# State-space scan of a decoder block: units of 1024 columns in place of 512, overwritten in place

## The reference

```
# 1. Mamba (I = 512 channels, N = 16 states)
hs, gate = split(x @ in_proj_w.T);  u = silu(conv4(hs) + conv_b)
dt, B, C = rmsnorm of the parts of u @ x_proj_w.T;  dt = softplus(dt @ dt_proj_w.T + dt_proj_b)
h[t] = exp(dt[t] * A) * h[t-1] + dt[t] * u[t] * B[t]      # per channel and state
y[t] = sum over states of h[t] * C[t];  y = (y + u * D) * silu(gate);  out = y @ out_proj_w.T
# 2. mLSTM over ctx_1024, 4 heads, gates from cumulative sums, norm over each head
# 3. feed-forward graph of 6 nodes, each with edge matrices q, k, v and attention of 8 heads
q, k, v = ew * (nodes @ We + be);  nodes[c] = act_w * (attention(q, k, v) @ Wo) + q
```

## Time and profile before

| | us |
|---|---|
| median of 3 runs | 1309.74 (1309.69 to 1315.06) |
| the profiled execution | 1308.01 |
| its span, first to last instruction | 1306.2 |
| TensorE busy | 1098.0 (84%) |
| VectorE busy | 1053.6 (81%) |
| ScalarE busy | 720.6 (55%) |
| mean granted TensorE clock | 0.939 of 2.4 GHz |

### The profile page before, as it was taken

How to read it: one execution, slowest core, us unless ns; L and a number is a source line. 1 busy time by engine, 2 the same in 40 slices (tenths; PEclk the granted TensorE clock), 3 DMA queues, 4 the chain that set the end, 5 groups by cost and what they waited for, 6 DMA issues and landing times. The chain is left out here.

```text
span 1306.2 us, 27811 instructions
## 1 busy us (share of the span) xinstructions
PE 1098.0 (84%) x11504; PEld 822.0 (63%) x11504; DVE 1053.6 (81%) x1683; ACT 720.6 (55%) x1692; POOL 2.9 (0%) x10
## 2 busy tenths in 40 slices
PE   3845668988999899989988998899888988897886
PEld 2723445766676667666666666666666666676665
DVE  2289887799999999999999999999999889725112
ACT  1434532576657665776567556755576646444332
POOL 0000000000000000000000000000000000000000
PEclk9767775999999999999999999999999989999998
DMA  6440343004100410030112211030104000000000
GB/s 190 122 178 32 107 153 113 33 3 130 41 26 33 132 42 25 34 105 28 50 49 62 71 50 49 16 117 33 58 3 130 33 25 34 2 1 10 2 1 9
DMA packets 53710, 76.14 MB, mean 58 GB/s; under 512 B 15376, under 2 KB 38672, under 8 KB 53456
## 3 DMA queue, kind: packets, MB, share of 16 engines
q1 hardware_dynamic: 53584, 74.37, 17.9%
HBM read 63.60 MB, written 10.75 MB: 57 GB/s over the span
## 5 line engine op out<-in xcount | busy, mean ns | idle before, releaser
L979 DVE TENSOR_TENSOR_SCAN unit_buf<-dec,unit_buf 128x512 f32<-128x512 f32 x256 | 311.9, 1218 | 11.7 <-ACT dec L753 11.0
L753 ACT ACTIVATE dec<-dts,a_neg 128x254 f32<-128x254 f32 x512 | 225.6, 499 | 42.5 <-DVE unit_buf L979 37.3
L972 DVE TENSOR_TENSOR unit_buf<-dtus,bs 128x512 f32<-128x512 f32 x256 | 175.0, 686 | 6.3 <-DMA dtus<-dt_rows 2.5
L990 DVE TENSOR_TENSOR unit_buf<-unit_buf,cs 128x512 f32<-128x512 f32 x256 | 175.3, 685 | 0.5
L1087 DVE TENSOR_REDUCE mx<-heads 128x16 f32<-128x2048 f32 x48 | 109.2, 2276 | 50.1 <-PE heads L602 50.0
L487 PE MATMUL ps<-unit_buf,fold 128*32 128x256 f32 x1024 | 89.0, 420 | 52.4 <-DVE unit_buf L990 52.3
L825 ACT ACTIVATE pr<-heads 128x512 f32<-128x512 f32 x192 | 99.1, 603 | 49.0 <-PE heads L617 49.0
L571 PE MATMUL ps<-node,wq_f 128*128 128x256 f32 x384 | 93.6, 387 | 7.8 <-ACT node L840 7.8
L640 PE MATMUL heads<-node,we_f 128*128 128x256 f32 x384 | 94.7, 389 | 0.0
L647 PE MATMUL heads<-aT,wo_f 128*128 128x256 f32 x384 | 93.7, 387 | 0.9 <-DVE aT L1096 0.9
L581 PE MATMUL heads<-wv_f,node 128*128 128x256 f32 x384 | 91.8, 382 | 0.0
(11 more groups left out here) (178 smaller groups left out, 1777.8 us busy)
## 6 DMA issues: line engine op xcount, KB each, us to landing
dts<-dt_rows SPq DMA_DIRECT2D x32, 512.0 KB, 3.8
dtus<-dt_rows SPq DMA_DIRECT2D x32, 512.0 KB, 5.2
node<-in_w_edgeT SPq DMA_DIRECT2D x18, 256.0 KB, 3.6
dt_rows<-dt SPq DMA_DIRECT2D x32, 128.0 KB, 2.4
dt_rows<-th SPq DMA_DIRECT2D x32, 128.0 KB, 2.5
bs<-bc_rows SPq DMA_DIRECT2D x32, 128.0 KB, 4.6
cs<-bc_rows SPq DMA_DIRECT2D x32, 128.0 KB, 4.3
xin<-in_x SPq DMA_DIRECT2D x8, 256.0 KB, 6.2
```

The source lines that it names most:

```text
L753: last = fn(dec[k % 2][:, a, :, 1:L], dts[c % 2][:, blk, :].rearrange("p (b t) -> p b t", b=GB)[:, :, 1:L], ACT.Exp, scale=a_neg[:, c, blk ...
L972: v.tensor_tensor(inf[k % 2][:], dtus[c % 2][:, 2 * pair:2 * pair + 2, :], bs[:, q:q + 1, :].broadcast_to([P, 2, T]), ALU.mult).then_inc(s ...
L979: v.tensor_tensor_scan(hst[k % 2][:].rearrange("p a b -> p (a b)"), dec[k % 2][:].rearrange("p a b t -> p (a b t)"), inf[k % 2][:].rearran ...
L990: v.tensor_tensor(prd[(i * UNITS + k) % PRDS][:], hst[k % 2][:], cs[:, q:q + 1, :].broadcast_to([P, 2, T]), ALU.mult).then_inc(sig["outflo ...
```

## The change

A unit becomes all four blocks of one set: 4x256 = 1024 columns. There are 4 units a chunk and 16 a group. Input, states and product share one tile: feed writes `ring[k % 3]`, scan overwrites it with the states, weigh overwrites those with the product, and the fold reads it. So feed of unit k waits until the fold of unit k-3 is done, and the waits of scan and weigh for free buffers are gone. `unit` k on VectorE is now weigh k-1, feed k+1, scan k. ScalarE makes four instructions of decays for a unit; `dec` has two buffers of 1024 columns. The fold is one for each unit, with the same matmuls as one for two before. The four tables are new.

```diff
-CUNITS = NGRP * BLKS // 2
+CUNITS = NGRP
-PRDS = 5
+RING = 3
...
-    if _k >= 2 and _k % 2 == 0:
-        U_STEPS += [("u", "add", _k // 2 - 1)]
+    if _k >= 1:
+        U_STEPS += [("u", "add", _k - 1)]
...
-A_AT = [-90, -86, -76, -69, -62, -58, -57, -52, -44, -43, -42]
+A_AT = [-101, -88, -76, -75, -62, -58, -56, -52, -49, -43, -42]
...
-        dec = [sb(f"dec{j}", [P, 2, GB, L]) for j in range(2)]
-        unit_buf = sb("unit_buf", [P, 4 + PRDS, 2 * T])
-        inf, hst, prd = ([unit_buf[:, j].rearrange("p (a n) -> p a n", a=2) for j in slots]
-                         for slots in ((0, 1), (2, 3), range(4, 4 + PRDS)))
+        dec = [sb(f"dec{j}", [P, BLKS, GB, L]) for j in range(2)]
+        ring = [sb(f"ring{j}", [P, BLKS, T]) for j in range(RING)]
...
-                    after(sp, used, i - 1, UNITS - CUNITS + 2 * q + 2)
+                    after(sp, used, i - 1, UNITS - CUNITS + q + 1)
...
-            def add(i, j):
-                c, q = j // NGRP, j % NGRP
+            def add(i, k):
+                c, q = k // CUNITS, k % CUNITS
                 if q == 0:
                     after(pe, "y_read", i, c)
-                after(pe, "outflow", i, 2 * j + 2)
-                for k in (2 * j, 2 * j + 1):
-                    for a in range(2):
-                        r0 = SD * (k % 2 * 2 + a)
-                        last = mm(MY[r0:r0 + SD, 0:T], fold[:], prd[(i * UNITS + k) % PRDS][:, a, :],
-                                  start=(q == 0), stop=(q == NGRP - 1), tile_position=(0, r0))
+                after(pe, "outflow", i, k + 1)
+                for blk in range(BLKS):
+                    last = mm(MY[SD * blk:SD * (blk + 1), 0:T], fold[:], ring[(i * UNITS + k) % RING][:, blk, :],
+                              start=(q == 0), stop=(q == NGRP - 1), tile_position=(0, SD * blk))
...
                 after(act, "state", i, k - 1)
-                for a in range(2):
-                    blk = 2 * pair + a
-                    last = fn(dec[k % 2][:, a, :, 1:L],
+                for blk in range(BLKS):
+                    last = fn(dec[k % 2][:, blk, :, 1:L],
...
             def feed(i, k):
-                after(dve, "state", i, k - 1)
-                v.tensor_tensor(inf[k % 2][:], dtus[c % 2][:, 2 * pair:2 * pair + 2, :],
-                                bs[:, q:q + 1, :].broadcast_to([P, 2, T]), ALU.mult).then_inc(sig["inflow"], 1)
+                after(dve, "ysum", i, k - RING + 1)
+                v.tensor_tensor(ring[(i * UNITS + k) % RING][:], dtus[c % 2][:],
+                                bs[:, q:q + 1, :].broadcast_to([P, BLKS, T]), ALU.mult).then_inc(sig["inflow"], 1)
             def scan(i, k):
+                states = ring[(i * UNITS + k) % RING][:].rearrange("p k t -> p (k t)")
                 after(dve, "decay", i, k + 1)
                 after(dve, "inflow", i, k + 1)
-                after(dve, "outflow", i, k - 1)
-                v.tensor_tensor_scan(hst[k % 2][:].rearrange("p a b -> p (a b)"),
-                                     dec[k % 2][:].rearrange("p a b t -> p (a b t)"),
-                                     inf[k % 2][:].rearrange("p a b -> p (a b)"), 0.0, ALU.mult,
+                v.tensor_tensor_scan(states, dec[k % 2][:].rearrange("p k b t -> p (k b t)"), states, 0.0, ALU.mult,
                                      ALU.add).then_inc(sig["state"], 1)
             def weigh(i, k):
+                states = ring[(i * UNITS + k) % RING]
                 after(dve, "state", i, k + 1)
-                after(dve, "ysum", i, (k - PRDS) // 2 + 1)
...
+                v.tensor_tensor(states[:], states[:], cs[:, q:q + 1, :].broadcast_to([P, BLKS, T]),
+                                ALU.mult).then_inc(sig["outflow"], 1)
...
             def unit(i, k):
                 if k == 0:
                     feed(i, 0)
+                if k >= 1:
+                    weigh(i, k - 1)
                 if k + 1 < UNITS:
                     feed(i, k + 1)
-                if k >= 1:
-                    weigh(i, k - 1)
                 scan(i, k)
```

29 lines of the change are left out of this document (13 added, 16 removed).

## The result

The changed kernel takes 1314.53 us in the median of 20 runs (1312.73 to 1321.43), the kernel before 1309.77 in the same comparison: ratio 1.0038, interval 1.0028 to 1.0048. It is slower by 0.4%, within what the prediction called no change; forecast were 1286 us and a gain. The profiled execution took 1313.7 us.

What follows compares the result with a forecast made beforehand. VectorE, nearly full in six of eight periods, was taken as the bound. Savings of 17.4 us over six periods, 5.5 at the start and 1.0 in the last but one made 23.9 off 1308.0; median forecast 1286, range 1278 to 1294.

Steps and rivals of the forecast that it cites:

- The multiplies: On VectorE, merging two 512-column multiplications saves about 0.075 us by distance of starts; 32 merges a group, 2.4 us.
- the scan: On VectorE, a 1024-column scan takes 2310 ns; each merge saves 0.04 us, 0.7 us a group.
- the dependent start: VectorE instructions waiting for the scan just issued start 0.12 us later; fewer such places save 0.9 us a group.
- Rival B: VectorE's fixed instruction cost counts in full, 7.7 us a group, but TensorE's 133.0 us limit cuts: 1272 us; chance 0.12.
- In place at zero: VectorE scans overwriting their own tile cost nothing extra; bounds zero and 1.9 us a group, no gain expected.
- New waits, 1.1 us a group, at the ring: VectorE feeds wait for TensorE's folds to free one of three tiles, 1.0 us a group; wide units delaying TensorE, 0.1.
- Period 137.3-4.0+1.1 = 134.4: Steady period: VectorE's 4.0 us saving taken off in full, 1.1 us of new waits added; six periods give 17.4 us.
- TensorE's floor of 133.0: Steady period if VectorE never held TensorE up, with TensorE's own work and waits for ScalarE unchanged: 133.0 us.
- ScalarE at nothing: Four decay exponentials for one wide unit have the same cover from VectorE's work as before, so no cost.
- Start, -5.5: Before the first feed-forward: 6.0 us from wide units plus 2.5 from the norm, less 3 at weight preparations: 5.5 us less.
- C: Slower: the ring of three ties the engines together, 9.0 us of waits a group against 4.0 gained: 1334 us; chance 0.10.
- D: No change: new waits eat the gain in the periods, weight preparations eat the start's: 1308 us; chance 0.08.

Runs made afterwards that it cites:

- e15: Kernel before with input, states and product of each 512-column unit in one tile overwritten in place, nine tiles; order, tables, widths unchanged: 1306.3 us, ratio 0.9971 to before.
- e2: Changed kernel's wide units and ring of three, but at the slots of the four old tables: 1614.4 us, ratio 1.2328 to before.
- e1: Changed kernel, same order and tiles, with each of a unit's three VectorE instructions issued as two of 512 columns: 1329.7 us, ratio 1.0153 to before.
- e17: Kernel of e16 with each merged multiplication again as two of 512 columns, at the places the merge gave them: 1322.6 us, ratio 1.0085 to before.
- e3: Changed kernel with each scan over only the first 512 of its 1024 columns (work left out): 1295.4 us, ratio 0.9889 to before.
- e4: Kernel before with each scan over only the first 256 of its 512 columns (work left out): 1283.2 us, ratio 0.9791 to before.
- e9: Changed kernel with two dummy TensorE products ahead of each of two waits, the dt projection's second half and the last head's values: 1310.4 us, ratio 1.0030 to before.
- e11: Changed kernel with each of ScalarE's decays computed for only the first half of a sequence (work left out): 1310.1 us, ratio 1.0000 to before.
- e18: Kernel of e15 in a ring of four, with only the two weighings of a pair merged, at the second one's place: 1324.6 us, ratio 1.0103 to before.
- e6: Changed kernel with all four slot tables rewritten: feeds moved by 1 to 6 slots, two folds and the weight preparations later: 1328.7 us, ratio 1.0133 to before.
- e8: Changed kernel with one number of the mLSTM table changed, the last head's scores at slot 57 instead of 58: 1345.2 us, ratio 1.0270 to before.
- e10: Changed kernel with the weight preparations' slot table taken back to that of the kernel before: 1334.8 us, ratio 1.0184 to before.
- e16: Kernel of e15 in a ring of four, with the two multiplications of a pair of units merged to 1024 columns, scans narrow: 1315.4 us, ratio 1.0048 to before.

## Why the prediction was wrong

- *The multiplies, the scan, the dependent start:* right. Starts 1.13 apart; scan 2285 ns for 2310 forecast, the dependent product 2.32 us behind it (550.54 to 552.86). Behind a wide scan an instruction that doesn't wait starts after 2.20 us, for 2.22 forecast. VectorE's busy time fell 3.4 us a period, for a forecast of 4.0. Rival B, the fixed cost in full, falls with the starts. By the Trainium skill ("VectorE: DVE Perf Modes", section on the TRN2 errata) the fixed cost lies between instructions, and the starts would be 1.22 apart, an estimate from its figure; the trace has 1.13 and disagrees.
- *The page's busy sum, -54:* it fell 29.3. I took it for a sum of durations; where starts overlap ends it is not, it is their union. The three groups' own sums fell by 662.2-603.6 = 58.6 us.
- *In place at zero:* not slower, right; but e15 is 0.6 us a period faster (0.4 between periods without a fall of the clock), and the dependent start is the difference that its trace shows, even without wider units.
- *New waits, 1.1 us a group, at the ring:* wrong in kind. No feed waited for a fold, and in e2, which is 304 us slower, only one did, 2.1 us. What the ring and the pairs cost lay in the order, with the falls of the clock that it brings: 3.0 us a period in e1, 2.9 in e17 against e15.
- *Period 137.3-4.0+1.1 = 134.4:* **this step failed.** It took VectorE's saved time off the period in full because VectorE was nearly full. e3 and e4 show what time saved on VectorE was worth there: 0.5 and 2.2 us for 17.5. A near-full engine was no bound; three engines in fixed orders waited for single answers of each other, and those answers moved with the tables. Measured, the period is 138.3: e1's places +3.0, the width -2.1. And TensorE's clock stood nowhere in the sum: its falls make most of the step from 137.4 to 138.3, and e9's period without them, 137.2, is what the saving of 3.4 us on VectorE came to.
- *TensorE's floor of 133.0:* it took TensorE's waits for VectorE as the only ones that could go, and its own work and the others as fixed. In the changed kernel the waits for VectorE stayed (16.9 us for 17.2 in four periods, at other places), those for key copies rose from 7.1 to 13.5 us, TensorE's idle time was 65.5 us for 66.1 in five periods, and its own work took 4.9 us longer at the lower clock.
- *ScalarE at nothing:* too low. Scans wait 6.4 us for decays (before 2.2), 1.0 a period more, and e11 gives 1.4 a period.
- *Start, -5.5:* the first keys did start earlier, 237.84 against 240.03 us, 2.2 of the 5.5. But they took 3.78 us, at 1.2 GHz, where they had taken 1.99, and the first group ended 4.1 us later. The granted clock of that stretch is 0.96 for 1.00.
- *Last two stretches, -1:* they gave 2.8.
- Rivals: C named slower and a coupling, but its mechanism, the ring, is not what e1 to e18 show; D (1308) came nearest to 1314.5 us, and that is in part luck: it had the gain eaten by new waits and the start by the preparations, where TensorE's clock took most of what was lost.

**What stays open.** Which of the moved places costs how much in the changed kernel: all three changes to its tables (e6 all four, e8 one step, e10 one table) made it slower, which doesn't tell what any single slot costs. How much of e1's, e16's, e17's and e18's loss is waiting and how much is clock; no run parts the two there. And why the first keys come at 1.2 GHz; e10 changed the preparations ahead of them and the keys at 255.01 us were slow too (3.57). Ahead of the fast keys of before TensorE had a block of the Mamba input (L452, 3.47 us from 235.25), ahead of the slow ones only products of one column (L424, L404); that this decides is not shown.

## What to carry to other kernels

Before saved time on a busy engine is counted, ask what that engine's time is worth in each stage, by a kernel that leaves half of its largest instruction out: here 12 to 15 of 44 us up to the first group's end, almost nothing in the steady periods. Where several engines run in orders written out by hand, merging two instructions moves one of them, and that place can cost three times what the merge gives; take first what moves nothing, as working in place with a ring did here. And before a lower clock is called a companion of waits, compare periods of one execution with and without a fall, and look at all executions and not at their mean alone.

## What the runs showed of the hardware

A multiplication of 1024 columns in place takes 1218 ns and so does one that isn't; a scan of 512 takes 1216 ns in place (e15) and 1218 otherwise, and the wide one in place 2285. Neighbouring instructions of VectorE start some 0.08 to 0.09 us before the last one's recorded end, at 512 and at 1024 columns, so that merging two multiplications gives 0.075 us and not the fixed part of the durations, 0.15 us; in e1 two narrow ones in a row take 1.20 us from start to start for 1.13 of the wide one. An instruction that waits for the one just ahead on VectorE loses 0.12 us (1.25 for 1.13 behind a narrow scan, 2.32 for 2.20 behind a wide one), and a ring in which it needn't wait removes that without any width (e15). A fall of TensorE's clock to 1.2 GHz for 3.4 us made a period 1.3 to 1.7 us longer in the changed kernel (138.7 and 139.1 for 137.46).
